# Attention row sums over one accumulator instead of two, completed by a DMA and GpSimd in the next unit

## The reference

```python
def heads(y):
    return y.reshape(B, L, H, HD).transpose(0, 2, 1, 3)      # B=2, L=2048, H=16, HD=32
q = heads(x @ Wq + bq); k = heads(x @ Wk + bk); v = heads(x @ Wv + bv)
scores = jnp.einsum('bhqd,bhkd->bhqk', q, k) / np.sqrt(HD)
attn = jax.nn.softmax(scores, axis=-1)
out = jnp.einsum('bhqk,bhkd->bhqd', attn, v)
```

## Time and profile before

| | us |
|---|---|
| median of three runs (3072.29 to 3077.43) | 3072.98 |
| the profiled execution's own time | 3068.99 |
| its span, first to last instruction | 3067.6 |
| PE busy in the span | 3035.4 |
| DVE busy | 2130.2 |
| POOL busy | 1546.5 |
| ACT busy | 1385.3 |

### The profile page before, as it was taken

One profiled execution on the slowest core, in us unless ns is written; L12 is line 12 of the kernel. 1 busy time (PEld: TensorE's weight loads), 2 busy tenths in 40 slices (PEclk: granted clock), 3 DMA queues, 4 the chain that ended last, 5 costly groups with the idle time before them and its releaser, 6 DMA issues.

```text
span 3067.6 us, 42811 instructions
## 1 busy us (share of the span) xinstructions
PE 3035.4 (99%) x16090; PEld 2113.4 (69%) x16090; DVE 2130.2 (69%) x3627; ACT 1385.3 (45%) x2673; POOL 1546.5 (50%) x655
## 2 busy tenths in 40 slices
PE   7999999999999999999999999999999999999999
PEld 5887655555555555555555546788888888789998
DVE  5557889899998989999899978643333323236666
ACT  3221566666666666666666673321111111022332
POOL 0000588989889898888989884300000000102222
PEclk9999999999999999999999999999999999999999
DMA  7683787978879788797977867620011110311221
GB/s 238 203 255 120 178 170 166 199 151 190 172 166 200 149 190 172 164 201 150 195 169 157 180 146 243 226 76 14 28 42 42 41 42 16 110 64 59 89 79 67
DMA packets 169374, 423.36 MB, mean 138 GB/s; under 512 B 18501, under 2 KB 60613, under 8 KB 141872
## 3 DMA queue, kind: packets, MB, share of 16 engines
q0 software_dynamic: 27744, 201.08, 32.3%
q1 hardware_dynamic: 139648, 214.04, 23.1%
q10 hardware_dynamic: 1776, 5.51, 0.7%
HBM read 143.47 MB, written 75.50 MB: 71 GB/s over the span
## 4 chain that ended last, share of the span: by engine, by line
PE 94%; DMA 2%; DVE 2%; issue 1%; POOL 1%; ACT 0%; SPq 0%; DVEq 0%; ACTq 0%; POOLq 0%
PE ps L414 16%; PE ps L727 15%; PE ps L738 15%; PE ps L1262 12%; PE ps L1249 11%; PE ps L510 5%; PE ps L1817 4%; PE ps L514 3%; PE ps L1834 3%; PE ps L744 2%; PE ps L1854 1%; PE ps L1604 1%; PE ps L158 1%; PE ps L1109 1%; DMA x<-in_x 1%
## 5 line engine op out<-in xcount | busy, mean ns | idle before, releaser
L427 DVE TENSOR_REDUCE nmp<-ps 128x1 f32<-128x512 f32 x1966 | 1199.7, 680 | 108.9 <-PE ps L414 104.1
L817 ACT ACTIVATE pt<-ps 128x512 f32<-128x512 f32 x2048 | 1030.9, 628 | 457.3 <-PE ps L727 454.4
L916 POOL TENSOR_TENSOR pt<-pt 128x2048 f32<-128x2048 f32 x217 | 995.0, 4585 | 120.0 <-ACT pt L817 114.8
L727 PE MATMUL ps<-qs,ks 128*128 128x512 f32 x2048 | 810.9, 400 | 2.0 <-ACT pt L817 2.0
L414 PE MATMUL ps<-ks,qs 96*128 96x512 f32 x1966 | 804.3, 409 | 0.1
L414 PEld LDWEIGHTS ps<-ks,qs 96*128 96x128 f32 x1966 | 373.3, 190 | 264.8 <-DVE nmp L427 166.4
L738 PE MATMUL ps<-pt,vq 128*32 128x512 f32 x4096 | 492.5, 598 | 0.0
L727 PEld LDWEIGHTS ps<-qs,ks 128*128 128x128 f32 x2048 | 389.4, 191 | 95.1 <-ACT pt L817 18.5
L1249 PE MATMUL ps<-hpb,w 128*128 128x512 f32 x1536 | 381.4, 398 | 0.0
L1262 PE MATMUL ps<-w,gp 128*128 128x512 f32 x1536 | 379.1, 395 | 1.3 <-DVE gp L1378 1.3
L1262 PEld LDWEIGHTS ps<-w,gp 128*128 128x128 f32 x1536 | 288.7, 188 | 70.3 <-DVE gp L1378 2.1
(11 more groups left out here) (179 smaller groups left out, 2789.5 us busy)
## 6 DMA issues: line engine op xcount, KB each, us to landing
pt<-pt POOLq DMA_DIRECT2D x189, 1024.0 KB, 8.4
qk_d<-st SPq DMA_DIRECT2D x128, 256.0 KB, 3.0
qs<-qk_d SPq DMA_DIRECT2D x87, 256.0 KB, 4.9
ks<-qk_d SPq DMA_DIRECT2D x42, 512.0 KB, 8.3
xina<-in_x SPq DMA_DIRECT2D x8, 1024.0 KB, 6.7
v_d<-vst SPq DMA_DIRECT2D x32, 256.0 KB, 3.1
vq<-v_d SPq DMA_DIRECT2D x32, 256.0 KB, 4.1
ao_d<-accs SPq DMA_DIRECT2D x32, 256.0 KB, 6.9
```

The costliest lines, as they stand in the source:

```text
L427: dve.tensor_reduce(nmp[:, n // 4, n % 4:n % 4 + 1], ps[:, ring.bank["max", u], :], AX.X, ALU.max, negate=True).then_inc(s_mr, 1)
L727: pe.matmul(ps[:, score_bank(n), :], ksb[w % 2][:, hh, 128 * kt:128 * kt + 128], qsb[:, v % 3, hh, :], start=True, stop=True).then_inc(s_s ...
L817: act.activation(pt[:, exp_slot(g), hh, :], ps[:, score_bank(n), :], ACT.Exp, scale=SCALE).then_inc(s_exp, 1)
L916: pool.tensor_tensor(accumulator(v, 0), accumulator(v, 0), pt[:, exp_slot(g), :, :], ALU.add).then_inc(s_add, 1)
```

## The change

The two accumulators that PE summed become one. In the next unit, at tile 3, POOL waits for the last two accumulating DMAs of the unit before and issues one more, which adds accumulator 1 into accumulator 2 (new, 30 times in all, for units 0 to 29). At tile 9 of that unit POOL adds accumulator 2 into accumulator 0 (`pool_merge`, earlier done behind tile 15 of the unit itself) and then does `pool_values`, which stood behind tile 5. PE's `pe_sums` moves from phase 2 to phase 6 and has one set of products instead of two. DVE's copy moves from phase 3 to phase 7, its reciprocals to one piece in each of phases 0 to 3, and the store of the output from phase 4 to phase 6, in front of the extra query row. Keys are fetched in phases 1 and 3 of the first three units of a group instead of phases 1, 3 and 4 of the first two. Units 30 and 31 keep the sums of before.

```diff
+def sums_phase(v):
+    return 6 if v < NU - 2 else 2
...
+            if v >= NU - 2:
+                pe.wait_ge(s_dma[0], dma_count(v, 0, dma_tiles(v, 0)[-1]))
+                pe_ones(bank, accumulator(v, 1), not last, False)
+            if last:
+                pe.wait_ge(s_add, add_count(v, added_tiles(v)[-1]))
+            else:
+                pe.wait_ge(s_mg, v + 1)
+            pe_ones(bank, accumulator(v, 0), v < NU - 2, True).then_inc(s_end, 1)
...
-                if v >= 2 and f < 3:
+                if v >= 2 and v < NU - 1 and f < 4:
+                    dve_recip(v - 2, (f,))
...
+        def pool_merge(v):
+            whole = dma_count(v, 1, dma_tiles(v, 1)[-1]) + (16 if v < NU - 2 else 0)
+            pool.wait_ge(s_dma[1], whole)
+            pool.wait_ge(s_add, add_count(v, added_tiles(v)[-1]))
+            pool.tensor_tensor(accumulator(v, 0), accumulator(v, 0), accumulator(v, 2), ALU.add).then_inc(s_mg, 1)
...
+                if 0 < v < NU - 1 and kt == 3:
+                    for d in range(2):
+                        pool.wait_ge(s_dma[d], dma_count(v - 1, d, dma_tiles(v - 1, d)[-1]))
+                    pool.dma_start(accumulator(v - 1, 2), accumulator(v - 1, 1), accum_op=ALU.add).then_inc(s_dma[1], 16)
...
-                if v < NU - 1 and kt == 15:
-                    ...
+                if v == NU - 2 and kt == 15:
+                    pool_merge(v)
+                if 0 < v < NU - 1 and kt == 9:
+                    pool_merge(v - 1)
-                if kt == 5 and v >= 2:
+                if kt == (5 if v == NU - 1 else 9) and v >= 2:
                     pool_values(v - 2)
...
-                if f == 4 and v >= 2:
+                if f == (4 if v == NU - 1 else 6) and v >= 2:
                     sp_store_ao(v - 2)
...
-                if v + NCH - c < NU and c < 2 and f in (1, 3, 4):
-                    i = 3 * c + (1, 3, 4).index(f)
+                if v + NCH - c < NU and c < 3 and f in (1, 3):
+                    i = 2 * c + f // 2
```

More of the change, by code:

```diff
@@ L64, in dma_count @@
 def dma_count(v, d, kt):
-    return 16 * (len(ADD_DMA[d]) * v + dma_tiles(v, d).index(kt) + 1)
+    return 16 * (len(ADD_DMA[d]) * v + d * min(v, NU - 2) + dma_tiles(v, d).index(kt) + 1)
 def add_count(v, kt):
-    return (len(ADD_POOL) + 1) * v + added_tiles(v).index(kt) + 1
+    return len(ADD_POOL) * v + added_tiles(v).index(kt) + 1
+def sums_phase(v):
+    return 6 if v < NU - 2 else 2
 def exp_slot(g):
@@ L103, in __init__ @@
                     self.use(("max", EARLY - 2 + 8 * p + i))
-            if f == 2 and v:
+            if v and f == sums_phase(v - 1):
                 self.use(("sums", v - 1))
@@ L277, in program @@
         s_dma = [sem(f"s_dma{i}") for i in range(2)]
-        (s_sc, s_exp, s_pv, s_add, s_end, s_accs, s_accv, s_rec, s_an, s_on, s_wo) = (
+        (s_sc, s_exp, s_pv, s_add, s_end, s_accs, s_accv, s_rec, s_an, s_on, s_wo, s_mg) = (
             sem(n) for n in ("s_sc", "s_exp", "s_pv", "s_add", "s_end", "s_accs", "s_accv", "s_rec", "s_an", "s_on",
-                             "s_wo"))
+                             "s_wo", "s_mg"))
         def sp_load_ss(i, ns):
@@ L869, in dve_attention @@
                     dve_split_wo(f + 1)
-                if f == 3 and v:
+                if v and f == sums_phase(v - 1) + 1:
                     dve_sums(v - 1)
@@ L877, in dve_attention @@
                             dve_row_max(u // 64)
-                if v >= 2 and f < 3:
+                if v >= 2 and v < NU - 1 and f < 4:
+                    dve_recip(v - 2, (f,))
+                if v == NU - 1 and f < 3:
                     dve_recip(v - 2, ((0,), (1,), (2, 3))[f])
@@ L917, in pool_attention @@
                                        ALU.add).then_inc(s_add, 1)
-                if v < NU - 1 and kt == 15:
-                    pool.wait_ge(s_dma[1], dma_count(v, 1, dma_tiles(v, 1)[-1]))
-                    pool.wait_ge(s_add, add_count(v, 15))
-                    pool.tensor_tensor(accumulator(v, 0), accumulator(v, 0), accumulator(v, 2), ALU.add).then_inc(s_add, 1)
-                if kt == 5 and v >= 2:
+                if v == NU - 2 and kt == 15:
[3 more added lines that the diff above has]
+                if kt == (5 if v == NU - 1 else 9) and v >= 2:
                     pool_values(v - 2)
```

## The result

The changed kernel takes 3122.92 us (median of 4 runs, 3119.82 to 3125.4), the kernel before on the same chip 3073.4: a ratio of 1.0161, interval [1.0149, 1.0173]. It is 49.5 us slower, where 3070 was predicted, with a range that ended at 3092. The profiled execution took 3121.93 us, span 3120.6, mean granted clock 0.990 (0.998 before); against the profiled execution of before that is 52.9 us more.

A forecast was written before the change was run, and what follows sets the result against it. PE was taken to bound the kernel, with 94% of the span. -25.8 + 22 + 1.5 = -2.3 us gave 3066.7 from the profiled 3068.99; the median, 3.99 above that execution, was predicted at 3070, range 3046 to 3092.

The forecast's parts named there:

- One set less, -25.8: PE's row sums: one set of products fewer saves 0.86 us a unit in 30 units, -25.8 us.
- DVE, 0: DVE with one reciprocal in each of four phases: at worst 1 us behind in all, taken as 0.
- SP, 0: Output store ahead of the extra query row: row 1 to 2 us later, 8 us of cover, taken as 0.
- POOL's 31.5 us: POOL's work from tile 8's add through tile 15's, with merge and `pool_values`: 31.5 us, then the new DMA at 1010.6.
- keeps its beat: POOL reaches tile 3's DMA in time and keeps its beat; the new transfer goes out only 2 us ahead.
- 5.1 - 1.1 = 4.0 us pass on: DMA engines: the new transfer takes 5.1 us, 1.1 are free, so 4.0 pass on, first to tile 3's transfer.
- The rule of turns between queues: DMA engines alternate between queue rows after whole packets; tile 3's transfer would then pass waiting query and key transfers.
- 20 x 1.1 us: Waits at tile 9's exponential in 20 units with keys, 1.1 us each: +22 us; 0 for the ten others.
- the 0 of unit 14: Unit 14, tile 9's exponential: tile 3 was forecast to land just in time, 0 us late.
- and this time is lost: When tile 3 lands late, ACT stops, PE's scores stop three blocks later, and this time is lost.
- The end, +1.5: Units 30 and 31, where unit 30's merge comes some 3 us later against PE: between -2 and +4, taken as +1.5.
- the engines run out of time: Rival: DMA engines 94% loaded, lateness carries into the next unit's new DMA; 2.2 us in 20 units, +44, 3093; chance 0.27.

The follow-up runs named there:

- e1: The changed kernel without its 30 new DMAs, the row sums leaving out accumulator 1: 3050.0 us, ratio 0.9925 to the kernel before.
- e1b: The changed kernel without the 30 new DMAs and with PE's second set of sums back, in phase 6: 3074.7 us, ratio 1.0008 to the kernel before.
- The two edits against that wait: Changed kernel with tile 7's DMA issued behind tile 8's add: 3109.6 us; the same with POOL's merge right behind that DMA: 3106.9 us.
- e12: The kernel before, with tile 9's first exponential done two to five times more in units 1 to 29, an artificial wait: 3145.3 us, ratio 1.0241.
- e2: The changed kernel with its new DMA but without POOL's merge at tile 9: 3047.7 us, ratio 0.9915 to the kernel before.
- e10: Changed kernel with tile 9 in accumulator 1 of the unit before, tile 7's DMA behind tile 8's add, the merge right behind that: 3056.1 us.

## Why the prediction was wrong

- *One set less, -25.8*: right. Phases 2 and 6 give 0.86 us a unit, and e1 against e1b 24.7 us.
- *DVE, 0*: right. Phases 0 to 3 take 5.79 with a reciprocal in each.
- *SP, 0*: right. The store goes out 41 us into unit 13, the row 0.5 us behind it, and PE's first score waits for neither.
- *POOL's 31.5 us* from the add of tile 8 to the end of tile 15's: 31.8 in unit 13 (1001.55 to 1028.76 + 4.61). The new DMA went out 9.6 us into unit 14, forecast 10.0. But "keeps its beat" failed: the add of tile 8 began 29.0 us into the unit, forecast 25.8, behind the wait for tile 3. The two edits against that wait brought 13 and 16 us.
- *The DMA engines, "5.1 - 1.1 = 4.0 us pass on"*: the first step that failed, in its size. Without the new DMA tile 3 lands at 22.2 on the mean, with it at 27.3: all of the 5.1 us pass on. The free 1.1 us was read from a stretch that is 0.75 busy before the change; after it the engines are 0.94 busy ahead of the new DMA, and full from there on. And both transfers are on one queue, and the new one landed first in all 29 units. The rule of turns between queues that the prediction weighed (the Trainium skill, DMA: Bandwidth & Descriptors, "Queues, rings and completion order") concerns transfers on different queues and could not help tile 3 here. Overtaking does occur after the change, but against tile 3: in unit 13 the second transfer of keys, issued on the other queue at 987.90, 3.4 us behind tile 3's DMA, landed 8.8 us later, 3.7 us ahead of it. So it is in 18 of the 20 units with keys, and in none in e1. It is not what costs: in units without keys (v modulo 4 of 3) tile 3 lands 5.8 us later than in e1, on the mean, and 5.1 in all units.
- *"20 x 1.1 us"*: the step that set the sign. The mean over three units took in the 0 of unit 14, which loads no keys before the change but does after it, and then the units without keys were counted as 0 once more. Units 13, 14 and 17 were late by 2.4, 1.2 and 2.4 us (forecast 1.45, 0 and 2.2), and no unit with v modulo 4 of 0 was read, where it is 3.2 on the mean. Tile 9's exponential is 2.2 us late on the mean of the 20 units with keys, and 1.4 in the nine others of units 1 to 29. The waits cost 52.5 us in these, not 22.
- *"and this time is lost"*, a wait priced at its length: this was taken for granted and failed. In ten units the granted clock fell behind a wait, another 17.7 us; e12 shows it without the change.
- *The end, +1.5*: within the bounds given. Unit 30 takes 0.9 us less, unit 31 2.35 more, of them 2.01 for the merge of unit 30 (compare):

```profile
1883.85 1.06 PE L750 MATMUL ps<-pt,ones 128*32 128x512 f32 x8 [2.01 <-POOL pt L912]
```

- *The rivals*: "the engines run out of time" named the right place, the right waits (27; tile 9 is over 2 us late in fifteen units) and a loop that exists but is the smaller part; it gave 3093 and the wrong reason. e2 and e10 carry the whole transfer in units of 47.3 us: the engines have room for it, but here a landing with too little cover stood behind it. The wait hardly spread to tiles 11 and 13.

With the measured sizes the same sum reads: -25.7 (30 units) + 52.5 + 17.7 + 2.35 (unit 31) + 2.7 (phase 5, 0.09 in each of 29 units) - 0.5 (the other phases) + 1.8 + 2.2 = 53.1, against 52.9 measured.

## What to carry to other kernels

Before adding a transfer, look for the landing that has the least cover among those behind it on its queue, and compare the cover with the whole of the new transfer's time in every kind of unit; a part of the sum that rests on three readings needs one of each kind. A wait of PE can cost about twice its length, as the granted clock may fall behind it: here it did behind 10 of the 14 waits of 1.7 us and more, and behind 7 of 14 artificial ones of 2.1 and 2.7 us. If the cover is short, look at the buffer too: another slot for the one tile that waits, with two steps of POOL in another order, gave 3056.1 us, and moving the whole transfer behind tile 5's gave 3079.3.

## What was not expected of the hardware

- The granted clock fell to about half (0.56 for 3.9 and 0.50 for 4.9 us in the two units shown) behind waits of PE of 1.7 to 3.8 us, in 10 of the changed kernel's 29 units and in 7 of 29 with artificial waits; it stayed in other units with idle times of up to 3.1 us.
- POOL's adds take 4.58 us in quiet stretches and 4.8 to 5.5 where they follow a DMA issue of POOL at once (116 of them with the merges, in units 1 to 29; the mean of the adds is 4.90 over the changed kernel, 4.59 before). So a DMA can cost POOL more than its issue.
- A VectorE product of two SBUF operands stood for up to 15.6 us beside GpSimd's adds, 2.7 at the least (29 of them, median 12.8), where POOL does it in 1.6.
